# Weight sums kept in DRAM by the first batch, and the keys' pair placed behind the heads' pair

## The reference

```python
h = embed(x) + 8 * bias + pos                      # [4, 512, 1024]
qkv = layernorm(h) @ w_qkv.T                       # 32 + 8 + 8 heads of 128
scores = einsum("bskgd,btkd->bkgst", qh, kh) * scale   # causal, softmax
attn = einsum("bkgst,btkd->bskgd", probs, vh)
h = h + attn @ w_dense.T
t = layernorm(h)[:, perm]                          # 16 blocks of 64
h = h + (gelu(t @ up) @ down)[:, unperm]           # per block, 64 -> 256 -> 64
```

## Time and profile before

| | us |
|---|---|
| median of 3 runs | 3031.98 |
| lowest and highest | 3023.79, 3032.52 |
| profiled execution, its own time | 3021.79 |
| its span | 3019.9 |
| TensorE busy, of the span | 2636.7 (87%) |
| VectorE, GpSimd, ScalarE busy | 1859.9, 1516.9, 1387.1 |
| DMA | 222 MB, mean 74 GB/s |

### The profile page before, as it was taken

How to read it: one execution, slowest core, us unless ns; L and a number is a source line. 1 busy time by engine, 2 the same in 40 slices (tenths; PEclk the granted TensorE clock), 3 DMA queues, 4 the chain that set the end, 5 groups by cost and what they waited for, 6 DMA issues and landing times.

```text
span 3019.9 us, 44985 instructions
## 1 busy us (share of the span) xinstructions
PE 2636.7 (87%) x16416; PEld 2272.7 (75%) x16416; DVE 1859.9 (62%) x4132; ACT 1387.1 (46%) x3334; POOL 1516.9 (50%) x1206
## 2 busy tenths in 40 slices
...
DMA packets 112460, 222.09 MB, mean 74 GB/s; under 512 B 13490, under 2 KB 13490, under 8 KB 112244
## 3 DMA queue, kind: packets, MB, share of 16 engines
...
## 4 chain that ended last, share of the span: by engine, by line
PE 48%; issue 19%; DVE 16%; POOL 8%; ACT 8%; DMA 0%; DVEq 0%; ACTq 0%; POOLq 0%
PE fb L554 12%; PE fb L556 12%; PE fb L555 12%; POOL w_lo L1178 6%; DVE prob L954 4%; PE tp L575 2%; POOL w_raw L1172 1%; ACT w_hi L787 1%; PE sc L554 1%; PE sc L555 1%; PE sc L556 1%; PE sc L628 1%; PE fb L637 1%; DVE second_out L1001 1%; DVE sc L943 1%
## 5 line engine op out<-in xcount | busy, mean ns | idle before, releaser
L1178 POOL TENSOR_TENSOR w_lo<-w_raw,w_hi 128x512 fp32r<-128x512 f32 x928 | 1188.7, 1318 | 401.4 <-ACT w_hi L787 393.7
L554 PE MATMUL fb<-xn_hi,w_hi 128*128 128x256 f32 x2688 | 781.0, 291 | 76.1 <-POOL w_lo L1178 34.9
L555 PE MATMUL fb<-xn_lo,w_hi 128*128 128x256 f32 x2688 | 763.9, 284 | 0.0
L556 PE MATMUL fb<-xn_hi,w_lo 128*128 128x256 f32 x2688 | 763.6, 284 | 0.0
L787 ACT ACTIVATE w_hi<-w_raw 128x512 fp32r<-128x512 f32 x928 | 537.8, 630 | 193.8 <-DVE w_raw L1152 152.4
L554 PEld LDWEIGHTS fb<-xn_hi,w_hi 128*128 128x128 f32 x2688 | 518.7, 193 | 102.6 <-issue 41.9
L1167 POOL TENSOR_TENSOR w_raw<-w_raw 128x512 f32<-128x512 f32 x96 | 123.3, 1285 | 922.4 <-DVE w_raw L1152 922.4
L555 PEld LDWEIGHTS fb<-xn_lo,w_hi 128*128 128x128 f32 x2688 | 519.4, 193 | 0.0
L556 PEld LDWEIGHTS fb<-xn_hi,w_lo 128*128 128x128 f32 x2688 | 518.7, 193 | 0.0
L554 PE MATMUL fb<-at_hi,w_hi 128*128 128x512 f32 x992 | 398.9, 402 | 48.6 <-DVE hacc L1031 42.3
L555 PE MATMUL fb<-at_lo,w_hi 128*128 128x512 f32 x992 | 395.3, 398 | 0.0
...
## 6 DMA issues: line engine op xcount, KB each, us to landing
w_raw<-in_w_qkv SPq DMA_DIRECT2D x384, 256.0 KB, 2.6
w_raw<-in_w_dense SPq DMA_DIRECT2D x256, 256.0 KB, 2.6
...
```

What stands on the lines that cost most here:

```text
L554: pe.matmul(dst, a_hi, b_hi, start=first, stop=False)
L555: pe.matmul(dst, a_hi, b_lo, start=False, stop=False)
L556: return pe.matmul(dst, a_lo, b_hi, start=False, stop=last)
L1178: pool.tensor_tensor(w_lo[:, m % RW, :], w_raw[:, m % RW, :], w_hi[:, m % RW, :], ALU.subtract)\
```

## The change

Five things are changed.

1. Batch 0 stores the four sums of each of its 24 pairs in DRAM (`sums_kept`, 96 tiles of 256 KB): SyncE's `keep`, in the step in which the sums are made, behind that step's loads. The low part of such a tile, which overwrites it, waits for its store (`kept`). Batches 1 to 3 load these tiles like any other; VectorE and GpSimd make no sums there (the lists `sums` hold only pairs of batch 0).
2. The planner counts only batch 0's pairs as paired, each tile of later batches being due by itself; LANDING goes from 3.5 to 4.0; the first tiles are due at X0 instead of X3.
3. The tail of the units becomes `Qr0 K Km Kn Kr PV3 VT`: MID, STATS, MLP0, MLP, GATHER, EMBED and TURN. FIRST, and EARLY, which is the old MID and is used in g 1 to 4 of batch 0, keep PV3 ahead of K.
4. VectorE makes the low part of a pair's first result at the end of Qr and Kr instead of Qn and Kn, behind the addition that frees the bank.
5. In the MLP units O stands behind PV1 instead of behind P; the Z steps of STATS are spread over the unit and end before Q0; Y and H of MLP0 stand ahead of S0 or apart; START is reordered.

```diff
+EARLY = ("S0 D0 N0 D1 D2 D3 Ta0 S1 Tb0 E1 Q1 Qm1 N1 Qn1 Ta1 Qr1 Tb1 S2 E2 D4 D5 N2 D6 D7 PV0 Ta2 S3 Tb2 E3 PV1 Q0 N3 "
+       "Qm0 Ta3 Qn0 Tb3 PV2 Qr0 PV3 K Km Kn Kr VT")
 MID = ("S0 D0 N0 D1 D2 D3 Ta0 S1 Tb0 E1 Q1 Qm1 N1 Qn1 Ta1 Qr1 Tb1 S2 E2 D4 D5 N2 D6 D7 PV0 Ta2 S3 Tb2 E3 PV1 Q0 N3 "
-       "Qm0 Ta3 Qn0 Tb3 PV2 Qr0 PV3 K Km Kn Kr VT")
+       "Qm0 Ta3 Qn0 Tb3 PV2 Qr0 K Km Kn Kr PV3 VT")
-STATS = ("S0 D0 N0 D1 D2 D3 Ta0 S1 Tb0 E1 Q1 Qm1 N1 Qn1 Ta1 Qr1 Tb1 S2 E2 D4 D5 N2 D6 D7 PV0 Z0 Z1 Ta2 S3 Z2 Z3 Tb2 E3 "
-         "PV1 Q0 N3 Qm0 Ta3 Qn0 Tb3 PV2 Qr0 Z4 PV3 Z5 K Km Kn Kr Z6 VT Z7")
-MLP0 = ("S0 Y0 Y1 H0 N0 H1 H2 H3 D0 Ta0 S1 Tb0 E1 Q1 Qm1 N1 Qn1 Ta1 Qr1 Tb1 S2 H4 E2 H5 H6 H7 f D1 D2 N2 D3 D4 D5 p F D6 "
-        "D7 u0 u1 PV0 u2 u3 Ta2 PV1 Tb2 S3 E3 P o Q0 N3 Qm0 Ta3 Qn0 Tb3 PV2 Qr0 U0 U1 PV3 U2 U3 K Km Kn Kr VT")
-MLP = ("S0 q D0 N0 f D1 D2 D3 Ta0 S1 Tb0 E1 Q1 Qm1 N1 Qn1 Ta1 Qr1 Tb1 S2 E2 p F D4 D5 N2 D6 D7 u0 u1 PV0 u2 u3 Ta2 PV1 "
-       "Tb2 S3 E3 P o Q0 N3 Qm0 Ta3 Qn0 Tb3 PV2 Qr0 U0 U1 PV3 U2 U3 K Km Kn Kr VT")
+STATS = ("S0 D0 N0 D1 D2 D3 Ta0 S1 Tb0 E1 Q1 Qm1 N1 Qn1 Ta1 Qr1 Tb1 S2 E2 D4 D5 N2 D6 D7 Z0 PV0 Z1 Z2 Ta2 Z3 S3 Z4 Tb2 E3 "
+         "Z5 PV1 Z6 Z7 Q0 N3 Qm0 Ta3 Qn0 Tb3 PV2 Qr0 K Km Kn Kr PV3 VT")
+MLP0 = ("Y0 H0 Y1 H1 H2 H3 S0 D0 N0 D1 D2 Ta0 H4 S1 H5 Tb0 E1 Q1 Qm1 N1 Qn1 Ta1 Qr1 H6 Tb1 H7 S2 E2 f D3 D4 N2 D5 p F D6 "
+        "D7 u0 u1 PV0 u2 u3 Ta2 PV1 o Tb2 S3 E3 P Q0 N3 Qm0 Ta3 Qn0 Tb3 PV2 Qr0 U0 U1 K Km U2 U3 Kn Kr PV3 VT")
+MLP = ("S0 q D0 N0 f D1 D2 D3 Ta0 S1 Tb0 E1 Q1 Qm1 N1 Qn1 Ta1 Qr1 Tb1 S2 E2 p F D4 D5 N2 D6 D7 u0 u1 PV0 u2 u3 Ta2 PV1 o "
+       "Tb2 S3 E3 P Q0 N3 Qm0 Ta3 Qn0 Tb3 PV2 Qr0 U0 U1 K Km U2 U3 Kn Kr PV3 VT")
...
-LANDING, PACE = 3.5, 1.4
+LANDING, PACE = 4.0, 1.4
...
-            steps += unit((MLP0 if g == 1 else MLP) if b else MID, b, g)
+            steps += unit((MLP0 if g == 1 else MLP) if b else EARLY, b, g)
...
+                kept = 4 * (3 * s.g + {"Q0": 0, "K0": 1, "Q1": 2}[f"{s.kind}{s.i}"]) - 1
                 for k, a in enumerate(A_USED):
-                    self.tiles.append(("qkv", blocks[a]) if a in blocks else ("sum", a))
+                    if s.b > 0 and a[0] == "S":
+                        self.tiles.append(("kept", kept + int(a[1])))
+                    else:
+                        self.tiles.append(("qkv", blocks[a]) if a in blocks else ("sum", a))
...
-            paired = user.kind not in JOBS
+            paired = user.kind not in JOBS and user.b == 0
...
-            if m < len(A_USED):
-                n = self.at[Step("X", 0, 0, 3)] + m
+
+            needed = m + 5 - k if paired else m
+            if needed < RW:
+                n = self.at[Step("X", 0, 0, 0)] + m
             else:
-
-                freed = self.at[self.user[(m + 5 - k if paired else m) - RW][0]]
+                freed = self.at[self.user[needed - RW][0]]
...
+            def keep(m):
+
+                n = pair[user[m][0]]
+                for k, a in ((2, "S2"), (4, "S1"), (3, "S3"), (6, "S4")):
+                    which = int(a[1])
+                    sp.wait_ge(w_sum12 if which < 3 else w_sum34, 2 * n + 2)
+                    sp.dma_start(sums_kept[4 * n + which - 1], w_raw[:, (m + k) % RW, :]).then_inc(kept[which - 1], 16)
...
+                if name == "kept":
+                    sp.wait_ge(kept[index % 4], 16 * (index // 4 + 1))
...
                 for m in tally.loads[s]:
                     sp.wait_ge(*used(m))
                     load(m)
+                for m in sums[s]:
+                    keep(m)
...
                     dve.tensor_tensor(second_out[:, 0:HALF], two[:, 0:HALF], second_out[:, 0:HALF], ALU.add)\
                        .then_inc(bank_free[bank(s)], 1)
-                    dve.wait_ge(split_hi, tally.high[s] + 1)
-                    dve.tensor_tensor(lo[:, own], second_out[:, own], hi[:, own], ALU.subtract).then_inc(first_low, 1)
                 elif s.kind in ("Qr", "Kr"):
...
                     dve.tensor_tensor(other[:, HALF:S], one[:, HALF:S], u2[:, :], ALU.add)\
                        .then_inc(bank_free[bank(s, 1)], 1)
+                    dve.wait_ge(split_hi, tally.high[s] + 1)
+                    dve.tensor_tensor(lo[:, own], second_out[:, own], hi[:, own], ALU.subtract).then_inc(first_low, 1)
...
             def low(m):
                 pool.wait_ge(w_rounded, m + 1)
+                s, k = user[m]
+                if s.kind not in JOBS and s.b == 0 and A_USED[k][0] == "S":
+                    pool.wait_ge(kept[int(A_USED[k][1]) - 1], 16 * pair[s] + 16)
```

More of the change, by code:

```diff
@@ L79 @@
+MLP0 = ("Y0 H0 Y1 H1 H2 H3 S0 D0 N0 D1 D2 Ta0 H4 S1 H5 Tb0 E1 Q1 Qm1 N1 Qn1 Ta1 Qr1 H6 Tb1 H7 S2 E2 f D3 D4 N2 D5 p F D6 "
+        "D7 u0 u1 PV0 u2 u3 Ta2 PV1 o Tb2 S3 E3 P Q0 N3 Qm0 Ta3 Qn0 Tb3 PV2 Qr0 U0 U1 K Km U2 U3 Kn Kr PV3 VT")
+MLP = ("S0 q D0 N0 f D1 D2 D3 Ta0 S1 Tb0 E1 Q1 Qm1 N1 Qn1 Ta1 Qr1 Tb1 S2 E2 p F D4 D5 N2 D6 D7 u0 u1 PV0 u2 u3 Ta2 PV1 o "
+       "Tb2 S3 E3 P Q0 N3 Qm0 Ta3 Qn0 Tb3 PV2 Qr0 U0 U1 K Km U2 U3 Kn Kr PV3 VT")
 GATHER = ("S0 q D0 N0 D1 D2 D3 Ta0 S1 Tb0 E1 Q1 Qm1 N1 A Qn1 Ta1 Qr1 Tb1 S2 E2 D4 D5 N2 G0 D6 D7 G1 PV0 Ta2 S3 Tb2 E3 G2 "
-          "PV1 Q0 N3 Qm0 G3 Ta3 Qn0 Tb3 PV2 Qr0 PV3 K Km Kn Kr VT")
+          "PV1 Q0 N3 Qm0 G3 Ta3 Qn0 Tb3 PV2 Qr0 K Km Kn Kr PV3 VT")
@@ L81 @@
 EMBED = ("S0 B0 D0 N0 D1 B1 D2 D3 Ta0 B2 S1 Tb0 E1 Q1 Qm1 N1 Qn1 Ta1 Qr1 B3 Tb1 S2 E2 D4 D5 N2 D6 D7 B4 PV0 B5 Ta2 S3 "
-         "Tb2 E3 B6 PV1 Q0 N3 Qm0 Ta3 Qn0 Tb3 PV2 Qr0 B7 PV3 K Km Kn Kr VT")
+         "Tb2 E3 B6 PV1 Q0 N3 Qm0 Ta3 Qn0 Tb3 PV2 Qr0 B7 K Km Kn Kr PV3 VT")
 TURN = ("S0 La4 D0 N0 Lb4 D1 D2 D3 Ta0 S1 Tb0 E1 Q1 Qm1 N1 Qn1 Ta1 Qr1 Tb1 X0 S2 X1 M0 E2 X2 D4 X3 D5 N2 X4 D6 X5 D7 X6 "
-        "PV0 Ta2 S3 X7 Tb2 E3 X8 M1 PV1 X9 X10 X11 X12 X13 Q0 N3 Qm0 Ta3 Qn0 Tb3 PV2 Qr0 PV3 K Km Kn Kr VT")
+        "PV0 Ta2 S3 X7 Tb2 E3 X8 M1 PV1 X9 X10 X11 X12 X13 Q0 N3 Qm0 Ta3 Qn0 Tb3 PV2 Qr0 K Km Kn Kr PV3 VT")
```

14 lines of the change are left out of this document (8 added, 6 removed).

## The result

| | before | after |
|---|---|---|
| median of 3 runs, us | 3031.98 | 2903.50 |
| lowest and highest | 3023.79, 3032.52 | 2899.20, 2906.65 |
| profiled execution, its own time | 3021.79 | 2906.65 |
| its span | 3019.9 | 2904.7 |

The changed kernel takes 0.9583 of the time of before, 95% interval 0.9551 to 0.9615. By the medians that is 128 us less where 75 were forecast; execution against profiled execution it is 115 us, since the one of before was 10 us under its median and the one of after 3 us above. The sum of the waits is worked on the profiled executions, so 115 is what it has to be held against, and 40 us are missing from it.

The account below looks back on a forecast made before the run. TensorE, busy 87% of the span, was taken as the bound, so only its ended waits gain. Terms -45 -22 +16 +32 -24 -16 +13 -27 -2 gave -75 us: 2947 profiled, scaled to 2957; range 2918 to 3003.

Parts of the forecast that it names:

- Part 5: D3's wait for hacc behind N0 in nine plain MLP units: 3.03 us falls to 1.3, -16 us.
- The new waits of the same kind, +13: D3 in the 11 other full units: a new wait for hacc of 1.2 us each, +13 us.
- Rival C: VectorE/GpSimd port lock slows N0 in all 24 later units; D3 or D2 waits 3.03 us each: 3005 us, chance 0.14.
- rival B: The sum, but with N0 free and S2's wait covered: some 2896 to 2930 us, chance 0.10.
- Part 1: Keys' pair before PV3 with ready tiles, batches 1 to 3: -45 us in 12 places, -22 in 12 MLP units.
- Part 2: Batch 0, LANDING 4.0 moves sums to Qr0: K 2.65 us later in 7 units, stores free, together +16 us.
- Part 3: q_lo behind L1010 makes S2 wait: +1.0 us in each of 32 units, +32 us.
- Part 4: O moved behind PV1 in MLP units: Q0's 12 waits for O's eviction, 21.1 us, and refills go, -24 us.
- Part 6: Unit after the statistics: Y0's row_buf and H's hacc waits shrink, 9 us a batch, -27 us.
- START -2: Reordering of START: -2 us, bounds -8 to +5.
- The listed signs: VT, K and Q0 freed of named waits; K over 5 us in batch 0; S2 about 1 us; 24 L1167/L1172 pairs.
- the two signs against it: Forecast wrong if N0 takes 5 us everywhere, or if K waits for w_lo in batch 1.

Follow-up runs that it names:

- the tiles alone: Kernel before with batch 0's sums kept in DRAM and loaded later, all orders old, later batches' tiles planned at 4.0 us: 2987.0 us, ratio 0.9872.
- the order alone: Kernel before with all new orders and the moved low part, sums made in every batch, LANDING 3.5: 3016.3 us, ratio 0.9968.
- the version without the new tail there: Changed kernel with batch 0's paired tiles at 3.5, q_lo of Q1 in Qn1, PV3 ahead of K outside the twelve MLP units: 2826.4 us, ratio 0.9350.
- Repaired: Changed kernel with batch 0's paired tiles planned at 3.5 and PV3 ahead of K in its GATHER and EMBED: 2874.5 us, ratio 0.9510.
- the other repair: Batch 0's paired tiles at 3.5, PV3 ahead of K in its GATHER and EMBED; with q_lo of Q1 in Qn1 too, changed kernel: 2853.9 us.

## Why the prediction was off, step by step

The direction was right and the size was not: the sum was 40 us short between profiled executions. Idle time fell by 102 us (383.2 to 281.4) and busy time by 13 (2636.7 to 2623.3), with 67 waits fewer; that is 0.2 us a wait, the refill that I had reckoned with. So nearly all of the 40 us are waits that I miscounted or didn't list. The clock was wrong in single terms, by 10 to 20 us, but what batch 0 loses by it the rest gains. By the sum's own steps:

**Part 5, D3's wait, -16: the term that failed.** It is the largest single miss. I counted nine units; the wait stands in twelve (g 2 to g 5 of three batches: 12 of the 21 waits of that line in the earlier trace rows). I left 1.3 us of it; none is left. And I priced it at its idle time, while behind it the clock fell: the unit of before has 84.16 us of busy TensorE at 0.98 where after has 81.50 at 1.00. Gone are 12 x 3.03 = 36 us, 12 refills of 0.17, and, in eight of the twelve, about 1.5 us of clock: some 50 us instead of 16. That is what its going is worth, not what the missing sums alone did: with the tiles alone, planned at 4.0, D3 still waits 0.73 us (1.96 in g 5), and with the order alone, sums and all, the wait is gone as well. Either half takes most of it, which neither my sum nor a list of parts can share out. The unit of before as a window, and N0 and GpSimd in it:

```profile
1049.62:1141.08 91.46, 84.16 (x515) 69.86 (x514) 57.12 (x123) 45.44 (x107) 48.79 (x39) 0.98 0.25 75
...
1058.47 1.28 POOL L1167 TENSOR_TENSOR w_raw<-w_raw 128x512 f32<-128x512 f32 x1 [3.14 <-DVE w_raw L1152]
1059.72 1.29 POOL L1172 TENSOR_TENSOR w_raw<-w_raw 128x512 f32<-128x512 f32 x1
1061.09 4.03 POOL L1178 TENSOR_TENSOR w_lo<-w_raw,w_hi 128x512 fp32r<-128x512 f32 x3
...
1058.50 5.48 DVE L954 TENSOR_SCALAR prob<-prob,inv_sum 128x128 f32<-128x128 f32 x4
```

and after:

```profile
1067.30 3.34 DVE L976 TENSOR_SCALAR prob<-prob,inv_sum 128x128 f32<-128x128 f32 x4
1070.56 1.46 DVE L1053 TENSOR_TENSOR hacc<-hacc,fb 128x512 f32<-128x512 f32 x2
...
1067.65 2.71 POOL L1203 TENSOR_TENSOR w_lo<-w_raw,w_hi 128x512 fp32r<-128x512 f32 x2 [1.56 <-ACT w_hi L809]
```

Before, N0 ran beside four instructions of GpSimd and took 5.48 us; after, it starts 0.35 us ahead of a pair of them and takes 3.34. Measured from S0 it starts 0.6 us sooner, so D1's addition comes 2.7 us sooner, and D3 just meets it. One multiplication takes 0.29 to 0.35 us alone and 1.33 to 1.51 beside GpSimd, all four before and two of four after. The Trainium skill, "SBUF — State Buffer", section "Who interferes with whom", lets a VectorE tensor_scalar in a two-port mode and a GpSimd instruction exclude each other for a whole instruction; the trace agrees in these durations, though it doesn't tell the mode. No run takes GpSimd away from N0 and leaves all else, so it stays a reading of the rows. The new waits of the same kind, +13, were right in size: five of 2.38 us.

**Rival C**, this lock in all 24 units, didn't happen where I feared it, and **rival B**, N0 free, was the better description of the MLP units. I gave B 0.10 because of S2, which was then right too (0.87 us, 29 times). That the measured time lies in B's range, 2896 to 2930, is luck as far as S2 goes: B had its wait covered.

**Part 1, the tail, -67: a total that comes near, for the wrong reason.** In batches 1 to 3 the waits that it lists (at_lo, w_lo, prob) go from 63 us in 66 waits to 2 in 11, and new ones for first_out and h_tok take back some 14; with the refills, and the place at the end of batch 0, that is 60 or so. K's bank wait is 0.52 us where I had 0.7, and VT's wait went. But I credited -45 us to the twelve places outside the MLP. Those gains come from ready tiles with either tail: with the tiles alone at 4.0 the units g 5, 6 and 7 of batch 1 go from 86.7, 86.2 and 105.1 us to 77.5, 82.5 and 100.5, and the version without the new tail there is 27 us faster. In the MLP units, where I had 1.8 us each, the tail is worth 5.5 in most, since with ready tiles the old tail makes U2 wait for ScalarE. I compared the old tail without ready tiles with the new tail with them, and never asked what the old tail would do with ready tiles. I also left out waits of the g 5 units that are gone after (Qm0 for u, 2.2 us, and 0.6 and 0.9 ahead of Ta2 and Ta3): g 5 went from 86.7 to 76.1 us.

**Part 2, batch 0, +16:** its profiled length grew by 35.5 us, of which some 8 are Part 3. K waits 5.14 us in the five plain units, 7.27 us in g 5 and 7.04 in g 6, as worked out from the earlier trace rows. TensorE's idle time grew by 16.7 us, the busy time by 18.8: at each of these waits the granted clock goes to half for a stretch, and that term was not in the sum at all. Repaired, batch 0 gives 29 us back. The stores cost nothing: with the tiles alone at 4.0, where batch 0 has the stores and the old orders, its plain units take 78.4 to 78.6 us and K waits 1.51 us for w_lo, as before. What I missed altogether is that LANDING also decides the later batches: I priced its change in batch 0 alone, where it costs, and it is worth 64 us in the others.

**Part 3, +32:** the wait is 0.87 us in 29 units, as forecast (1.0 in 32). Taken back it returns 13 us (21 beside the other repair), so part of it covered later waits. **Part 4, -24:** 35 by the run, 21 of idle time, as forecast, and 17 of busy time between the profiled executions. **Part 6, -27:** 31 by the run. START -2: -5.

Added up from separate runs: tiles at 4.0 -37, O -35, Z, Y and H -31, tail -42, batch 0 +29, low part +13 make -103, with START -108, against -115 to -128. The rest is interaction and noise, and not placed.

The listed signs came out: VT without a wait for VectorE's last addition in batches 1 to 3, K waiting 0.5 us for its bank, over 5 us for w_lo in batch 0, 0.9 us ahead of S2, Q0 not waiting for O. Neither of the two signs against it appeared.
